# Blank rows behind each expert's used slots, and flat conditions in the expert code

## The reference, cut to what matters

```python
x = x + L0_ffn(L0_cond(x, itok_B_0_7, ...), U, V, W1, b1, W2, b2)
x = x + L1_ffn(L1_cond(x, itok_B_0_15, L1_cond_W, L1_cond_b), ...)
# in L1_ffn: N = 2048, E = 64, TOP_K = 6, C = 2 * ceil(N * 6 / 64) = 384
pos = jnp.arange(A) - offsets[se]        # rank of the choice within its expert
valid = pos < C
buf = jnp.zeros((E, C, D)).at[se, pos_c].add(where(valid, x[st], 0))
g = einsum('ecd,efd->ecf', buf, w_gate); u = einsum('ecd,efd->ecf', buf, w_up)
eo = einsum('ecf,edf->ecd', silu(g) * u, w_down)
y = zeros_like(x).at[st].add(eo[se, pos_c] * weight) + shared_swiglu(x)
```

## Time and profile before

| | us |
|---|---|
| median of 3 runs | 617.28 (615.86 to 621.86) |
| the profiled execution | 624.11 |
| its span, first to last instruction | 622.4 |
| PE busy | 508.2 |
| POOL busy | 330.0 |
| DVE busy | 313.9 |
| ACT busy | 188.1 |

### The profile page before, as it was taken

How to read it: one execution, slowest core, us unless ns; L and a number is a source line. 1 busy time by engine, 2 the same in 40 slices (tenths; PEclk the granted TensorE clock), 3 DMA queues, 4 the chain that set the end, 5 groups by cost and what they waited for, 6 DMA issues and landing times.

```text
span 622.4 us, 11506 instructions
## 1 busy us (share of the span) xinstructions
PE 508.2 (82%) x2483; PEld 364.2 (59%) x2484; DVE 313.9 (50%) x823; ACT 188.1 (30%) x398; POOL 330.0 (53%) x289
## 2 busy tenths in 40 slices
PE   0797299489899899979999879999789898999920
PEld 0443153253545355558888757788668776889710
DVE  8731164274866862254445526555265544555424
ACT  0111012011221211033444425454255444455410
POOL 8900050572474767603767635655465545656750
PEclk9997689689999999989999979999799999999975
DMA  6999999996794222238999969999699989899779
GB/s 205 365 390 393 358 393 404 392 363 212 239 309 143 110 84 112 101 98 212 234 231 227 238 134 219 229 213 252 148 205 239 249 220 229 196 243 227 146 148 307
DMA packets 92394, 146.55 MB, mean 235 GB/s; under 512 B 10824, under 2 KB 72120, under 8 KB 92280
## 3 DMA queue, kind: packets, MB, share of 16 engines
q1 hardware_dynamic: 61608, 83.30, 42.6%
q0 software_dynamic: 30672, 61.75, 38.5%
HBM read 81.18 MB, written 63.83 MB: 233 GB/s over the span
## 4 chain that ended last, share of the span: by engine, by line
PE 49%; SPq 19%; DMA 10%; issue 10%; DVE 7%; POOL 3%; ACT 1%; POOLq 0%; DVEq 0%
PE bank L1074 21%; PE bank L1095 7%; PE bank L1096 7%; SPq L356 5%; SPq L355 5%; DMA x_g<-in_x 4%; PE bank L1055 4%; POOL slot_rows L491 3%; PE bank L935 2%; DMA wt<-in_wdt 2%; SPq L392 2%; PE bank L885 2%; SPq L363 2%; DVE M L749 1%; PE bank L956 1%
## 5 line engine op out<-in xcount | busy, mean ns | idle before, releaser
L502 POOL DMA_INDIRECT acc<-sil,sids x64 | 99.3, 1552 | 89.2 <-ACT sil L597 57.8
L491 POOL DMA_INDIRECT slot_rows<-ctok,sli x96 | 95.2, 991 | 80.0 <-issue 27.7
L502 POOL DMA_INDIRECT acc<-OH,sids x63 | 97.6, 1549 | 53.6 <-ACT OH L597 19.3
L1074 PE MATMUL bank<-xgT,wb 128*128 128x192 f32 (+9 forms) x384 | 85.2, 375 | 15.1 <-issue 12.8
L1074 PEld LDWEIGHTS bank<-xgT,wb 128*128 128x128 f32 (+1 forms) x384 | 65.6, 198 | 29.2 <-issue 17.0
L1096 PE MATMUL bank<-wt,hh 128*128 128x256 f32 x254 | 75.5, 379 | 0.0
L849 DVE TENSOR_TENSOR hh<-sg,bank 48x384 f32<-48x384 f32 x64 | 35.6, 556 | 74.0 <-ACT sg L586 73.2
L1096 PEld LDWEIGHTS bank<-wt,hh 128*128 128x128 f32 x254 | 48.3, 190 | 6.6
L584 ACT ACTIVATE sg<-bank 128x384 f32<-128x384 f32 x64 | 31.4, 491 | 55.4 <-PE bank L1074 55.1
L597 ACT ACTIVATE sil<-bank,wcol 128x256 f32<-128x256 f32 x64 | 29.7, 474 | 53.1 <-PE bank L1096 51.7
L597 ACT ACTIVATE OH<-bank,wcol 128x256 f32<-128x256 f32 x64 | 29.8, 474 | 51.3 <-PE bank L1096 50.0
(11 more groups left out here) (185 smaller groups left out, 739.1 us busy)
## 6 DMA issues: line engine op xcount, KB each, us to landing
cw<-slot_rows SPq DMA_DIRECT2D x127, 136.0 KB
cw<-in_cW SPq DMA_DIRECT2D x64, 256.0 KB, 6.2
wb<-in_wblk SPq DMA_DIRECT2D x32, 496.0 KB, 4.1
slot_rows<-xgT POOLq DMA_DIRECT2D x12, 1088.0 KB, 15.9
slot_rows<-wb POOLq DMA_DIRECT2D x12, 1088.0 KB, 25.0
h0T<-in_wblk SPq DMA_DIRECT2D x16, 496.0 KB
hT<-in_wblk SPq DMA_DIRECT2D x16, 496.0 KB
acc<-zrow POOLq DMA_DIRECT2D x2, 2432.0 KB
```

What stands on the lines that cost most here:

```text
L491: pool.indirect_dma_start(slots_d, bass.IndirectOffsetOnAxis(sli[:, g % 2, k, t:t + 1], 0), ctok[:, g % 2, t, :], None, bounds_check=SLOTS ...
L502: pool.indirect_dma_start(acc[u % 2], bass.IndirectOffsetOnAxis(sids[:, u % SR, j:j + 1], 0), yo[u % UE][:, j, :], None, compute_op=ALU.ad ...
L1074: ins = mm(bank[o][0:m, 0:n], w(b, c), xgT[u % UE][:, c, 0:n], start=c == 0, stop=c == DC - 1)
```

## The change

The table is no longer zeroed. It now has 448 rows per expert (`SPACED`, 384 slots and 64 spare rows), one expert after the other, without blocks. When the counts are known, SP writes 64 blank rows right behind the last used slot of each expert (`fill`, the place from a new row of `facts`, `UNUSED`): 12 before it waits for the dispatch, the others in its steps, five experts ahead of the row loads. A row load waits for its expert's blank rows and covers the used rows rounded up to 64: each tile is loaded with 128 rows, 64 or not at all, and scattered likewise (`by_pieces`, which SP and POOL run for every tile as conditions in a line; `s_tick` is a semaphore that nobody waits for). `SIZES` becomes 64, 128, ... 384. On TensorE tiles 0 and 1 are always computed, gate and up 192 or 256 wide, and a third tile is a separate piece of 128 columns under one condition.

```diff
-RB = 16
-SLOTS = E * CAP
+H = P // 2
+SPACED = CAP + H
+SLOTS = E * SPACED
+UN = 16
-SIZES = [P, 3 * P // 2, 2 * P, 5 * P // 2, CAP]
+AHEAD = 5
+SIZES = [n * H for n in range(1, CAP // H + 1)]
...
-        blocks = slots_d.rearrange("(b e r) c -> e b r c", e=E, r=RB)
+        blank = sb("blank", [H, RW])
...
-        def by_tiles(eng, size, work):
-
-            with eng.If(size > THREE):
-                work(3)
+        def by_pieces(eng, size, work):
+
+            with eng.If(size > 0):
+                work(0, P)
             with eng.Else():
-                with eng.If(size > TWO):
-                    work(2)
+                work(0, H)
+            for j in range(1, TJ):
+                with eng.If(size > 2 * j):
+                    work(j, P)
                 with eng.Else():
-                    work(1)
+                    with eng.If(size > 2 * j - 1):
+                        work(j, H)
+                    with eng.Else():
+                        eng.sem_inc(s_tick, 1)
...
+            def fill(e, u):
+                sp.dma_start(slots_d[bass.ds(get(UNUSED, e, u), H), :], blank[:, :]).then_inc(s_unused[u % UN], 16)
+
+            for e in range(UE + 3 + AHEAD):
+                fill(e, e)
             for q in range(2):
                 sp.wait_ge(s_scat[q], 16 * TOPK * TG * G // 2)
-            get, start = notes(sp, 0)
 
             def loads(e, u):
-                def load(j):
-                    sp.dma_start(xg[:, u % UE, j, :], blocks[bass.ds(e, 1), j * P // RB:(j + 1) * P // RB].rearrange("a b r c -> (a b) r c")).then_inc(s_xg[u % UE], 16)
+                def load(j, rows):
+                    sp.dma_start(xg[0:rows, u % UE, j, :], slots_d[bass.ds(e * SPACED + j * P, rows), :]).then_inc(s_xg[u % UE], 16)
 
                 size = get(SIZE, e, u)
-                load(0)
-                with sp.If(size > TWO):
-                    load(1)
-                    with sp.If(size > THREE):
-                        load(2)
+                sp.wait_ge(s_unused[u % UN], (16 // UN) * (e - u % UN + UN))
+                sp.sem_inc(s_tick, 1)
+                by_pieces(sp, size, load)
...
                 if not (isinstance(e, int) and e >= E - UE - 3):
+                    if not (isinstance(e, int) and e >= E - UE - 3 - AHEAD):
+                        fill(e + UE + 3 + AHEAD, u + UE + 3 + AHEAD)
                     rows_free(e + 3)
                     loads(e + UE + 3, u + UE + 3)
...
-            pool.wait_ge(s_w, 16 * 8)
-            for b in range(CAP // RB):
-                pool.dma_start(slots_d[b * E * RB:(b + 1) * E * RB, :].rearrange("(n p) c -> p n c", p=P),
-                               blanks[b % len(blanks)].unsqueeze(1).to_broadcast([P, E * RB // P, RW])).then_inc(s_init, 16)
...
-            pool.wait_ge(s_init, 16 * CAP // RB)
...
+                with pe.If(size > 3):
+                    gate_up(2 * P, CAP, False)
+                with pe.Else():
+                    pe.sem_inc(s_tick, 1)
+                with pe.If(size > 2):
+                    gate_up(0, 2 * P, True)
+                with pe.Else():
+                    gate_up(0, P + H, True)
```

More of the change, by code:

```diff
@@ L223, in program @@
         s_ws = sem("shared_weights_loaded")
-        s_init = sem("slot_tokens_initialised")
+        s_unused = [sem(f"unused_slots_filled{i}") for i in range(UN)]
         s_x = sem("x_loaded")
@@ L308, in get @@
                 if (what, u) not in known:
-                    known[what, u] = eng.value_load(facts[0:1, what, bass.ds(e, 1)], min_val=0, max_val=16 * (TJ * E + TJ))
+                    known[what, u] = eng.value_load(facts[0:1, what, bass.ds(e, 1)], min_val=0, max_val=SLOTS - H if what == UNUSED else 16 * (TJ * E + TJ))
                 return known[what, u]
@@ L441, in _ @@
             pool.memset(onesb[:, :], 1.0)
-            for blank in blanks:
-                pool.memset(blank, 0.0)
-            pool.iota(e_off_i[:, :], [[RB, E]], base=0, channel_multiplier=0)
+            pool.memset(blank[:, :], 0.0)
+            pool.iota(e_off_i[:, :], [[SPACED, E]], base=0, channel_multiplier=0)
             pool.iota(iota_i[:, :], [[1, E]], base=0, channel_multiplier=0)
@@ L458, in _ @@
                                pattern=[[-3, K0], [0, R0]], channel_multiplier=1)
-            for b, blank in enumerate(blanks):
-                last = pool.iota(blank[:, TOK:TOK + 1].bitcast(I32), [[0, 1]], base=N + b * RB, channel_multiplier=1)
-            last.then_inc(s_const, 1)
+            pool.iota(blank[:, TOK:TOK + 1].bitcast(I32), [[0, 1]], base=N, channel_multiplier=1).then_inc(s_const, 1)
             pool.wait_ge(s_const, 3)
@@ L509, in scatters @@
                 pool.sem_inc(s_tick, 1)
[L510 to L517, removed]
+                by_pieces(pool, size, scatter)
             def step(e, u):
@@ L779, in group @@
                     for i, n in enumerate(SIZES[:-1]):
-                        last = v.tensor_scalar(more[:, i, :], bank[6][:, 0:E], n + 0.5, None, ALU.is_ge)
+                        v.tensor_scalar(more[:, i, :], bank[6][:, 0:E], n + 0.5, None, ALU.is_ge)
+                    last = v.tensor_scalar(unused[:, :], bank[6][:, 0:E], float(CAP), None, ALU.min)
                     last.then_inc(s_fl, 1)
@@ L1046, in tokens @@
             def tokens(e, u):
[L1048 to L1052, removed]
-                    for c in range(DC):
[L1054 to L1058, removed]
@@ L1059, in tokens, with turn @@
[L1059 removed]
+                def turn(c, j):
+                    return tr(bank[c][:, j * P:(j + 1) * P], xg[:, u % UE, j, c * P:(c + 1) * P], ident[:, :])
+                gathered = get(GATHERED, e, u)
+                size = get(SIZE, e, u)
+                pe.wait_ge(s_xg[u % UE], gathered)
+                if u:
+                    pe.wait_ge(s_xs, e)
+                    pe.wait_ge(s_xv, e)
+                pe.sem_inc(s_tick, 1)
+                with pe.If(size > 3):
+                    for c in range(DC):
+                        turn(c, 2)
@@ L1061, in step, with gate_up @@
+                with pe.Else():
+                    pe.sem_inc(s_tick, 1)
+                for c in range(DC):
+                    turn(c, 0)
+                    turn(c, 1).then_inc(s_xp, 1)
             def step(e, u, first=False):
                 b = u % UE
[L1064 to L1071, removed]
+                def gate_up(lo, hi, told):
@@ L1077, in step @@
                 start(e, u)
-                by_rows(get(SIZE, e, u), gate_up)
+                size = get(SIZE, e, u)
+                pe.wait_ge(s_wb[b], (32 // UE) * (e - b + UE))
+                if isinstance(e, int) and e == E - 1:
+                    pe.wait_ge(s_xs, e + 1)
+                    pe.wait_ge(s_xv, e + 1)
+                if not first:
+                    pe.wait_ge(s_hh, 2 * e)
+                pe.sem_inc(s_tick, 1)
+                with pe.If(size > 3):
+                    gate_up(2 * P, CAP, False)
@@ L1084, in down, with tile @@
             def down(e, u):
[L1087 to L1109, removed]
+                def tile(j):
+                    o = bank[5 + j][:, 0:D]
+                    mm(o, hh[:, u % 2, 0, j * P:(j + 1) * P], down_first(u % UE), start=True, stop=False)
+                    return mm(o, hh[:, u % 2, 1, j * P:(j + 1) * P], wt[u % UE], start=False, stop=True)
+                size = get(SIZE, e, u)
+                if u == E - 1:
+                    pe.wait_ge(s_hh, 2 * e + 2)
+                pe.wait_ge(s_ys, 2 * e + 1)
+                pe.wait_ge(s_yv, e + 1)
+                pe.sem_inc(s_tick, 1)
+                tile(0).then_inc(s_dp, 1)
+                with pe.If(size > 3):
+                    tile(2)
                 with pe.Else():
-                    by_rows(size, work, lo, mid)
+                    pe.sem_inc(s_tick, 1)
+                tile(1).then_inc(s_dp, 1)
             pe.wait_ge(s_flags, 1)
```

34 lines of the change are left out of this document (20 added, 14 removed).

## The result

| | before | change |
|---|---|---|
| median (lowest to highest), us | 619.26 (615.86 to 621.86), 4 runs | 638.62 (634.79 to 642.16), 4 runs |
| the profiled execution / its span | 624.11 / 622.4 | 634.79 / 633.1 |
| PE busy | 508.2 | 529.2 |
| mean granted clock | 0.937 | 0.953 |

The change is slower, ratio 1.0315 with a 95% interval of 1.023 to 1.0399. A later pair of runs gave 1.0339 (1.0269 to 1.0408). The forecast was 625 in a range of 594 to 645, slower at 0.5. The measured median lies inside that range and outside the 612 to 630 that the forecast called its own.

A forecast was written before the change was run, and what follows sets the result against it. Late x loads beside the zeroing held the early groups; TensorE bound the expert phase, with SP close behind. Early -34 and phase +42 gave +8 us, 632 profiled and 625 as median, range 594 to 645, its own 612 to 630.

The forecast's parts named there:

- Part 1: Early groups: without the 24 zeroing transfers the first two groups take the undisturbed 36.66 us, a gain of 34 us.
- Part 2: Expert loop on SP: 52 blank-row stores at 1.4 us each add 73 us of SP time, their wait 5.
- Part 3: SP's row loads: issues 0.31 us cheaper without the 16-row blocks, -35 us; flat conditions cost +43 us.
- Part 4: TensorE in the expert phase: wider tiles and an extra piece add 24 us, lying under SP's time.
- Part 5: Expert-phase transfers: 2112 rows fewer in loads and scatter-adds, 4096 blank writes more, together about nothing.
- The sum: SP's work grows from 251 to 337 us and sets the pace; phase +42, early -34, total +8 us.
- SP's loop jump: Rival at SP's loop end: the longer body's jump stalls twice, +9 us, giving 634; chance 0.2.
- TensorE staying the bound: Rival in the expert phase: SP's added work stays under 44 us, result 587 to 607, middle 597; chance 0.2.
- Less early gain: Rival in the early groups: x is late from SP's issue order, only 14 us come back, 645; chance 0.06.
- dear issues: Rival on SP's queue: all row DMAs still cost 0.66 us to issue, +51 us, giving 676; chance 0.07.
- What would show it: Signs in the trace: SP's waits near zero, two-tile steps 5.5 to 5.9 us, row and blank issues at 0.35.

## Why the prediction was right

The mechanism was right: SP's queue had 44 us to spare, the blank stores spent them, and SP then set the pace. The size was right in SP's sum, in part because errors cancel, and low in the median.

**Part 1, zeroing, -34.** Right: 19.8 + 12.6 = 32.4 in the two groups, 34.7 at SP's first weight issue. The mechanism was shown by putting the zeroing back. The clock in them came to 0.95 and 0.96, not quite the 1.00 forecast, and SP's 16 issues take 24.31 us where I assumed 19.32, still inside the group of 37.98.

**Part 2, blank stores, 1.4 each, +73.** Right in the sum, wrong in its pieces. A store in the chain takes 1.42, but the issue is 0.498 and not 0.35 (none of the bounding rows was a store), and the register load 0.273 and not 0.44. The two errors of 0.15 and 0.17 cancel by luck. Taking the stores away gave 1.25 each, 65 us.

**Part 3, row loads.** Cheaper by 0.305 each, as taken: 0.352 instead of 0.657. The branches: what is left of +80 after +65 for stores, +5 for the wait (not measured by itself) and -35 for row loads is +45, forecast +43. That is a remainder; of it, 19 us were measured as the price of flat against nested, and the rest was measured by no run. The -35 is the medians' figure: in the kernel before, rows in line alone took only 23 to 27 us off SP's work. With that the remainder is 33 to 37, too close to the forecast's 43 for a measure that is good to some 10 us.

**Part 4, TensorE, hidden.** Right, shown directly: 0 under SP, 7 us without that cover.

**Part 5, transfers, nothing.** Right in this: the same stores on ACT's queue cost nothing that shows, and SP's extra register loads cost time with no transfer.

**The sum.** SP's work +86 forecast, +80 measured. The window grew by 46 and not 42, since SP kept 10.3 us of waiting where I had written "near zero". The profiled execution was to be 632 and is 634.79. In the medians the forecast was 14 us low, +8 where +19 was measured: I laid the whole 6.8 us between the profiled execution and the median of before on the change as well, and the change's own profiled execution lay on the other side of its median. That step, a single trace's offset carried over to another kernel, is the part of the forecast that failed in size.

**The rivals.** SP's loop jump: its mechanism is there, its price is not. The prediction read the jump off the record of the branch, 45 ns, and said that no row shows SP stalled. Behind that record SP loses 2.40 and 2.45 us in the change, on the chain that ended last, 4.85 in all. But the records of the kernel before have the same gap behind SP's two jumps, 4.18 and 4.51 us, with waits of 3.8 and 2.3 us for TensorE behind them. So the stalls were part of the 251 us of work from the start, and the longer body of 727 instructions added nothing to them; the 9 us of this rival did not come on top. That they would have brought the forecast nearer to the median is chance. POOL is the engine whose jump did change: from it to the sequencer's next instruction are 0.25 and 0.21 us with 322 instructions, 3.3 and 4.4 us with 642; POOL does not set the pace. The Trainium skill, Runtime: NRT & Kernel Launch, section Instruction fetch mechanics, gives the other engines two blocks of 256 and a fetch for a jump out of them. The trace agrees for POOL and for ACT (178 instructions, 0.2 us); SP's 325 and DVE's 292 are fewer than 512 and stall all the same in the kernel before (DVE 5.7 and 4.3 us). Whether a body's place in the blocks decides that is not tested. So the prediction's sentence that of five loop bodies only TensorE's stalls is wrong. TensorE staying the bound (597): refuted as it stood, for it needed SP's added work under 44 us and that was 80. With the stores on ACT the added work is 267 - 252 = 15, and the result is 597, which is also that rival's number. Less early gain and dear issues: refuted by the rows of the early groups and by the 0.35 of L403, though a store's issue did go half of the way.

**What would show it.** Two-load steps of 5.5 to 5.9: 5.81. "TensorE idle for weight transfers in most steps" was too much: 14 times, 22.5 us. "Blank issue at 0.35" was wrong as well: 0.498.

## What to carry to other kernels

Before adding small transfers to a loop, add up what the issuing queue does per step (register loads, register arithmetic, branches, issues) and compare it with its waiting in that stage: that waiting is all the cover there is, here 44 us, and 1.25 to 1.4 us for each of 52 stores spent it. Put such issues on an engine with slack in its own order; here one moved statement turned 3% slower into 4% faster. An edit that costs nothing under a bound (wider tiles) must be priced again when the bound goes. And look behind a branch's record, at the start of the next instruction, before calling a jump cheap.

## What the runs showed of the hardware

- The same row load of 128 x 272 floats is issued in 0.352 us from consecutive rows and in 0.657 from eight blocks of 16 rows; a store of 64 such rows takes 0.498.
- A register load on SP took 0.273 us here and 0.447 in the median of the kernel before, and 0.69 with the register work around it as an addition to the loop. With only the 16-row blocks taken out of the kernel before it took 0.268 and 0.270, so the slower load goes with the blocked row loads; how stays open.
- The record of a taken jump back is 45 to 50 ns on SP, POOL and ACT and 63 on DVE, whether the engine then stalls or not; on TensorE's queue the record itself holds the stall, 3.99 and 4.31 us over some 2400 instructions, hardly less than over 4200.
- The gap behind that record, before and in the change: SP 4.18 and 4.51 us (325 instructions), 2.40 and 2.45 (727); POOL 0.25 and 0.21 (322), 3.3 and 4.4 (642); ACT 0.2 in both (178).
- DVE's loop of 292 instructions shows 5.7 and 4.3 us behind its jump in the kernel before, and 0.25 and 0.21 in both traces of that kernel with its rows in line, where the list ahead of the loop is some operations shorter and the loop is the same. The cause is not tested.
